# Eight row scatters spread over four attention steps with two buffers, the first expert weights copied by VectorE, and no products of zeros in the prologue

## The reference

```python
mod = (_silu(L0_c) @ L0_wmod).reshape(L0_c.shape[0], 6, 1, -1)
sa, ca, ga, sb, cb, gb = (mod[:, 0], mod[:, 1], mod[:, 2], mod[:, 3], mod[:, 4], mod[:, 5])
h = _layernorm(x, axis=-1) * (1 + ca) + sa
x = x + ga * _L0_attn_ref(h, Wq, Wk, Wv, Wo, gamma, beta)      # causal softmax, 16 heads of 8
h = _layernorm(x, axis=-1) * (1 + cb) + sb
# ffn: bids = sigmoid(h @ conf_w.T + conf_b) * wealth; the 2 best of 8 experts;
#      weights = softmax of the two bids; each expert: (silu(h @ gate.T) * (h @ up.T)) @ down.T
x = x + gb * _L0_ffn_ref(h, conf_w, conf_b, gate_w, up_w, down_w, wealth)
```

## Time and profile before

| | us |
|---|---|
| median of 3 runs | 632.87 (631.29 to 634.27) |
| the profiled execution's own time | 636.49 |
| its span | 634.7 |
| PE busy | 565.4 (89%) |
| DVE busy | 471.2 (74%) |
| ACT busy | 405.9 (64%) |
| POOL busy | 244.1 (38%) |

### The profile page before, as it was taken

One profiled execution on the slowest core, in us unless ns is written; L12 is line 12 of the kernel. 1 busy time (PEld: TensorE's weight loads), 2 busy tenths in 40 slices (PEclk: granted clock), 3 DMA queues, 4 the chain that ended last, 5 costly groups with the idle time before them and its releaser, 6 DMA issues.

```text
span 634.7 us, 16553 instructions
## 1 busy us (share of the span) xinstructions
PE 565.4 (89%) x5257; PEld 424.8 (67%) x5258; DVE 471.2 (74%) x1592; ACT 405.9 (64%) x716; POOL 244.1 (38%) x328
## 2 busy tenths in 40 slices
PE   5778999999898998998998987999888999999940
PEld 3455565666465565564564546999887999999930
DVE  5898787899797787796896863687765666667636
ACT  4425787878777786786786775686534655655612
POOL 5401301133723615416326243456554333343326
PEclk9597999999999898998998996999989999999975
DMA  4442668432333232322323011111321211111138
GB/s 125 132 121 70 176 173 224 130 110 74 95 93 93 82 93 72 103 77 71 106 82 93 3 36 27 40 44 53 103 78 53 53 50 50 42 50 50 40 124 289
DMA packets 61511, 56.82 MB, mean 90 GB/s; under 512 B 11156, under 2 KB 55572, under 8 KB 61444
## 3 DMA queue, kind: packets, MB, share of 16 engines
q1 hardware_dynamic: 56548, 44.88, 25.5%
q0 software_dynamic: 4320, 8.99, 4.3%
q10 hardware_dynamic: 576, 2.10, 0.8%
HBM read 36.92 MB, written 18.45 MB: 87 GB/s over the span
## 4 chain that ended last, share of the span: by engine, by line
PE 75%; DVE 6%; DMA 5%; issue 4%; ACT 3%; another core or an unknown queue 2%; SPq 2%; POOL 1%; ACTq 0%; POOLq 0%; DVEq 0%
PE psN L962 18%; PE psO L565 11%; PE psO L973 9%; PE psT L546 7%; PE psN L531 6%; PE psT L548 5%; PE psN L533 4%; PE psM L573 2%; ACT probs L1090 2%; DMA probs<-expert_out 2%; PE psM L591 2%; DVE negm L1408 1%; PE psM L614 1%; PE psM L596 1%
## 5 line engine op out<-in xcount | busy, mean ns | idle before, releaser
L1408 DVE TENSOR_REDUCE negm<-psN 128x1 f32<-128x512 f32 (+3 forms) x352 | 211.4, 634 | 49.6 <-PE psN L533 48.7
L1090 ACT ACTIVATE probs<-psT 128x512 f32<-128x512 f32 x320 | 179.6, 595 | 56.0 <-PE psT L548 41.0
L962 PE MATMUL psN<-probs 128*128 128x128 f32 x1136 | 142.2, 279 | 3.0 <-ACT probs L1283 2.3
L962 PEld LDWEIGHTS psN<-probs 128*128 128x128 f32 x1136 | 135.8, 196 | 3.6 <-issue 3.5
L546 PE MATMUL psT<-qst_all,kst_all 74*128 74x256 bf16 (+2 forms) x384 | 100.9, 281 | 13.4 <-ACT probs L1090 12.0
L2146 POOL DMA_INDIRECT expert_out<-kst_all,dest x71 | 69.2, 975 | 112.2 <-DVE kst_all L1914 107.6
L531 PE MATMUL psN<-kst_all,qst_all 74*128 74x256 bf16 (+2 forms) x384 | 102.2, 283 | 6.8 <-DVE negm L1408 4.1
L565 PE MATMUL psO<-probs,vaug 128*32 128x512 f32 (+3 forms) x1024 | 97.0, 458 | 0.1
L533 PE MATMUL psN<-kst_all,qst_all 117*128 117x128 bf16 x512 | 92.9, 225 | 0.0
L1283 ACT ACTIVATE probs<-gu_w 128x1024 f32 x71 | 74.9, 1056 | 25.4 <-PE psN L962 21.5
L1890 DVE TENSOR_TENSOR probs<-probs,psN 128x512 f32<-128x512 f32 x71 | 48.7, 686 | 53.0 <-PE psN L962 27.9
(11 more groups left out here) (241 smaller groups left out, 743.2 us busy)
## 6 DMA issues: line engine op xcount, KB each, us to landing
qst_all<-q_parts_dram SPq DMA_DIRECT2D x96, 96.0 KB
kst_all<-k_parts_dram SPq DMA_DIRECT2D x96, 96.0 KB
kst_all<-dispatched SPq DMA_DIRECT2D x71, 66.0 KB
q_parts_dram<-qparts SPq DMA_DIRECT2D x24, 128.0 KB, 2.4
k_parts_dram<-kparts SPq DMA_DIRECT2D x24, 128.0 KB, 1.8
xall<-in_x SPq DMA_DIRECT2D x8, 256.0 KB, 3.4
gu_w<-in_gateT SPq DMA_DIRECT2D x4, 512.0 KB, 5.1
gu_w<-in_upT SPq DMA_DIRECT2D x4, 512.0 KB, 4.9
```

The costliest lines, as they stand in the source:

```text
L962: mm = pe.matmul(bank[par][:, c * P:(c + 1) * P], ew[par][:, half, c * P:(c + 1) * P], xgT[par], start=True, stop=True)
L1090: nc.scalar.activation(probs[:, g % 2, 512 * u:512 * (u + 1)], psT[:, u % TBANKS, :], ACT.Exp, scale=SOFTMAX_SCALE).then_inc(exp_done, 1)
L1408: nc.vector.tensor_reduce(dst, src, axis=AX.X, op=ALU.max, negate=True).then_inc(nat_done, 1)
```

## The change

Five edits:

1. Eight scatters of a batch are issued at eight places over four steps, `SCATTERS`: three in step g = 3 (before unit 0, after units 4 and 8), two in step 0 of the next batch, two in step 1, one in step 2. `rows` and `slots` get a second buffer, taken in turn by batches, and `dispatched` becomes two semaphores. Of batch 5, three scatters fall into step (7, 3) and five into the head of the expert stage (j = 1, 3, 5, 7 and 9).
2. The weights of the first expert tile are copied by DVE (`first_weights`) at the end of step (7, 3); PE waits for them by `ew_first`. ACT begins with tile 1.
3. ACT's table for silu is loaded before its last `keep_values` and no longer behind it.
4. The 112 products of zeros are gone.
5. The writing of `padrows` on DVE in step (7, 3) moves from behind the second layer norm's statistics to the step's start; four small tables move into the space of `xn`, with one wait on a transpose of batch 7 that lies two batches back.

```diff
-        rows = sb("rows", [P, TB, ROW])
+        rows = [sb(f"rows{i}", [P, TB, ROW]) for i in range(2)]
-        slots = sb("slots", [P, 2, TB], I32)
+        slots = [sb(f"slots{i}", [P, 2, TB], I32) for i in range(2)]
...
+        def dispatched_before(eng, b):
+            for i in range(2):
+                eng.wait_ge(dispatched[i], 16 * 2 * TB * len(range(i, b, 2)))
...
+        SCATTERS = ((3, 0), (3, 4), (3, 8), (0, 3), (0, 9), (1, 2), (1, 9), (2, 4))
+        IN_LAST = sum(g == G - 1 for g, _ in SCATTERS)
...
-            sp.wait_ge(dispatched, 16 * 2 * TB * FULL_B)
+            dispatched_before(sp, FULL_B)
...
-            keep_running(FILL_LOAD)
             for k in range(NAT):
                 nat(0, 0, k)
-                keep_running(FILL_UNIT)
-            keep_running(FILL_MAX)
             turn_max(0, 0)
...
-                pe.wait_ge(ew_ready, j + 1)
+                if isinstance(i, int) and j == 0:
+                    pe.wait_ge(ew_first, 1)
+                else:
+                    pe.wait_ge(ew_ready, j)
...
             h_norm(B - 2, (2, 3))
+            nc.scalar.preload_act_table(ACT.Silu)
             keep_values(B - 1, 3)
...
-            nc.scalar.preload_act_table(ACT.Silu)
             act.wait_ge(ew_in, 16 * 12)
             act.wait_ge(tiles_ready, 1)
             act.wait_ge(pv_done, TB * (STEPS - 1))
-            keep_weights(0, 0)
...
+            def first_weights():
+                dve.wait_ge(ew_in, 16 * 12)
+                dve.wait_ge(pv_done, TB * (STEPS - 1))
+                e = dve.value_load(tile_w_i[0:1, 0:1], min_val=0, max_val=NX - 1)
+                V.tensor_copy(ew[0].rearrange("p k f -> p (k f)"),
+                              gu_w[:, bass.ds(e, 1)].rearrange("p o k f -> p (o k f)")).then_inc(ew_first, 1)
...
-                if has_earlier(b) and rows_of(b) is rows:
-                    hold("pool", pool, dispatched, 16 * 2 * TB * b)
+                if 2 <= b < B - 1:
+                    pool.wait_ge(dispatched[b % 2], 16 * 2 * TB * (b // 2))
...
+            def scatter_at(b, g, unit):
+                i = SCATTERS.index((g, unit))
+                sent = b - 2 if g == 3 else b - 3
+                if has_batch(sent):
+                    if unit:
+                        pool.wait_ge(exp_done, UNITS * (4 * b + g) + unit)
+                    scatter(sent, i)
...
+                if j % 2 == 1 and IN_LAST + j // 2 < 2 * TB:
+                    scatter(L - 2, IN_LAST + j // 2)
```

More of the change, by code:

```diff
@@ L320, in rows_of @@
         def rows_of(b):
-            return rows_last if isinstance(b, int) and b == B - 1 else rows
+            return rows_last if b == B - 1 else rows[b % 2]
         yp = [probs[:, b // 4, b % 4 * 2 * TB * E:(b % 4 + 1) * 2 * TB * E].rearrange("p (k n e) -> p k n e", k=2, n=TB)
@@ L327, in slots_of @@
         def slots_of(b):
[L328 removed]
+            return slots_last if b == B - 1 else slots[b % 2]
+        def dispatched_before(eng, b):
+            for i in range(2):
+                eng.wait_ge(dispatched[i], 16 * 2 * TB * len(range(i, b, 2)))
         passed = {e: sem(f"passed_{e}") for e in ("sp", "pe", "dve", "pool")}
@@ L898, in _ @@
             pe.wait_ge(ones_in, 16)
-            def keep_running(n):
-                for _ in range(n):
-                    pe.matmul(psO[:, 0:P], zero_b[:], zero_b[:], start=True, stop=True)
-            keep_running(FILL_LOAD)
             for k in range(NAT):
                 nat(0, 0, k)
-                keep_running(FILL_UNIT)
-            keep_running(FILL_MAX)
             turn_max(0, 0)
@@ new lines, in scatter @@
+                                      rows_of(b)[:, n, :], None).then_inc(dispatched[b % 2], 16)
+            def scatter_at(b, g, unit):
[5 more added lines that the diff above has]
+                    scatter(sent, i)
+            def step(b, g):
+                if g == 0:
+                    if has_batch(b - 2):
+                        h_scale(b - 2)
+                    if has_batch(b + 1) and has_earlier(b):
+                        low(b + 1, qres, qparts, q_mid, q_parts)
+                    if has_batch(b - 2):
+                        h_shift(b - 2)
+                    scatter_at(b, g, 3)
+                    if has_batch(b + 1):
+                        low(b + 1, kres, kparts, k_mid, k_parts)
+                    scatter_at(b, g, 9)
+                elif g == 1:
+                    scatter_at(b, g, 2)
+                    if has_batch(b - 1):
+                        o_inv(b - 1)
+                    if has_batch(b - 2):
+                        count(b - 2)
+                    if b == 0:
+                        x_inv(slice(2, B), 3)
+                        x_shift(slice(2, B))
+                    scatter_at(b, g, 9)
+                elif g == 2:
+                    scatter_at(b, g, 4)
+                    if has_batch(b - 1):
+                        add_attn(b - 1)
+                elif g == 3:
+                    scatter_at(b, g, 0)
+                    scatter_at(b, g, 4)
+                    if has_batch(b - 1):
+                        h_inv(b - 1)
+                    scatter_at(b, g, 8)
```

60 lines of the change are left out of this document (15 added, 45 removed).

## The result

| | before | after |
|---|---|---|
| median of 5 runs | 632.87 us | 612.76 us |
| lowest to highest | 631.29 to 634.27 | 611.86 to 614.62 |
| profiled execution, its span | 636.49, 634.7 | 611.86, 610.1 |

The ratio is 0.9686, 95% interval 0.9659 to 0.9712: 20.1 us less, where 611 was forecast. The traces are compared with each other, so their differences add up to 24.6 and not to 20.1.

A forecast was written before the change was run, and what follows sets the result against it. PE's own work was taken as the floor, with PE idle or slow-clocked behind bursts of scatters. Terms 20.1 + 4.0 - 3.6 + 1.1 = 21.6 less took the 632.87 us median to 611.3, forecast 611, range 605 to 617 (0.62).

The forecast's parts named there:

- batches 2 to 7, bursts gone: Attention: without bursts of scatters PE runs at full clock with little idle time; 20.1 us less, bounds 22.6 and 0.
- start of the expert stage, tiles 0 to 2: First expert tiles: ACT's table load and weight copy 2.0, last burst 0.7, clock 1.3; in all 4.0 us less.
- head, tiles 3 to 11, five new pairs: Expert stage's head: five of batch 5's scatters join tiles' sends there; 3.6 us more, bounds 0 and 11.
- prologue and batch 0: Prologue: without the products of zeros DVE's waits before six maxima go; 1.1 us less.
- some 3 us: Attention: the spacing of moved scatters, at least three units of exponentials apart.
- the rival of 631: Attention: the pause belongs to the place in step 3, so spacing gains nothing; 631 us, chance 0.08.
- Half a lag left: Attention: spaced scatters beside SP's loads each still hold ACT 0.5 us, giving back 9; 620 us, chance 0.15.
- Every spaced scatter costs: Attention: each of 43 moved scatters holds PE 0.72 us, 31 in all; 642 us, chance 0.05.
- the tables of `padrows` move into DVE's wait for `add_attn`, at nothing either way: Before the expert stage: moving DVE's writing of these tables neither costs nor gains time.
- a pair costs 0.72: Expert stage's head: each send with a scatter costs 0.72 us, so five new pairs cost 3.6.
- 1.1 stays as the gain: Prologue: slower products between 40 and 45 us are covered by PE's wait until 48.89, keeping the 1.1 us gain.
- the clock stays low: Behind 49 us: without zeros the clock rises later, costing 1.8 us; 613 us, inside the forecast's range, not counted apart.

The follow-up runs named there:

- the second set: Follow-up runs of before and after unchanged and of two kernels adding bursts or scatters; before took 632.7 us in its one run here, after 613.4.
- the set with pauses: The second set, whose traces show "remote" waits of ACT and DVE of up to 5.2 us, called pauses.
- the sets without pauses: The first and third sets of follow-up runs; none of their eight traces has a pause, and before took 607.9 and 607.0 us.
- e_double_narrow: Kernel after with each of 40 spaced scatters sent a second time, the second writing 64 bytes per row, not 528; 605.3 us, 0.995 of before.
- the first set: Follow-up runs undoing one part of the change at a time; the kernel before took 607.9 us (17 runs).
- e_old_places: Kernel after with each batch's scatters back at the old places in two bursts, none in the head; 602.0 us, 0.989 of before.
- e_after_again: Kernel after, unchanged, timed again in the second set; 613.4 us, 0.967 of before.
- e_scatters_only: Kernel before with only the scatters' new places and the two buffers; 600.6 us, 0.988 of before.
- e_head_free: Kernel after with batch 5's five scatters taken out of the head, all eight in step (7, 3); 599.5 us, 0.984 of before.
- e_zeros_back: Kernel after with PE's 112 products of zeros back in the prologue; 599.8 us, 0.987 of before.
- e_zeros_again: Kernel after with PE's 112 products of zeros back, a second time, in the third set of runs; 601.0 us, 0.986 of before.
- e_act_first: Kernel after with the first tile's weights copied by ACT again, behind its table load; 604.7 us, 0.995 of before.

## Why the prediction was right, and where not

| term | forecast | traces of the result | traces of the second set |
|---|---|---|---|
| batches 2 to 7, bursts gone | -20.1 | -22.4 (258.3 to 235.9) | -19.8 (255.7 to 235.9) |
| start of the expert stage, tiles 0 to 2 | -4.0 | -3.3 (11.73 to 8.42) | -2.8 (11.54 to 8.73) |
| head, tiles 3 to 11, five new pairs | +3.6 | +0.9 (32.02 to 32.88) | +0.8 (31.97 to 32.82) |
| head, tiles 12 to 29 | 0 | 0.0 (62.68 both) | 0.0 (62.76 to 62.80) |
| prologue and batch 0 | -1.1 | -0.1 (86.64 to 86.54) | +3.5 (86.33 to 89.79) |
| batch 1 | 0 | -1.0 (39.53 to 38.55) | -0.2 (38.84 to 38.64) |
| from tile 30 on | 0 | +1.3 (143.8 to 145.1) | +1.4 (143.8 to 145.2) |
| sum | -21.6 | -24.6 | -17.1 |

The two pairs of traces lie on either side of the difference of the medians (-20.1 and -20.7), so a term is known no better than the two columns agree.

**The bursts.** The reading of the earlier trace rows was right for the condition in which the kernel was timed: three or four indirect DMAs in a row are followed by pauses of ACT and DVE, one alone is not, and the pause follows the burst to another place. In the first pair the term is 2.3 us short. Batches 2 to 5 came out at 39.5 to 39.7 and not 40.1, because I left each the 0.5 us of idle time that batch 1 had; that is 1.9. Batch 6 gained 0.4 less than forecast and batch 7 0.2 more, and 0.5 lies in the stretch from 382.54 to the first tile, which the earlier trace rows left out. In the second pair the term comes out at 19.8. One reading was wrong without harm: three units of exponentials are not "some 3 us" but 2.2 at the closest (scatters at 175.28 and 177.47 in the kernel after), so 2.2 us is already far enough.

From the rule of the Trainium skill (SBUF — State Buffer, "Who interferes with whom") I had worked out that a burst on POOL could not hold ACT, which made the rival of 631. In the set with pauses ACT waits behind the burst, wherever it stands, so that rival has fallen. Whether SBUF's ports have a part in it no run shows, and in the sets without pauses nothing speaks against the rule.

**Half a lag left** did not happen: PE stands at most 0.05 us a batch in batches 2 to 5. **Every spaced scatter costs** did not either: 0.50 us each was the point where it decides, and e_double_narrow ran sixteen a batch in 39.40 us, though in a set without pauses; with them it is the kernel after, with eight a batch in 39.52 to 39.71, that excludes it.

**The start of the expert stage.** The sum came near, -3.3 and -2.8 for -4.0, but partly by luck. PE's wait for ACT's copy is gone and the products ran at the full clock, as forecast. The step that failed is "the tables of `padrows` move into DVE's wait for `add_attn`, at nothing either way": they hold up the statistics, through them ACT's last norm, and behind it the `oT` for which PE waits 0.60. The wait that was to take them in (2.72 us ahead of the statistics at 378.03) came from the burst that stood before `add_attn` on POOL, and went with it: after, the statistics wait for nothing but DVE's own work. ACT's copy for tile 1, which I had named as late next, costs 0.21. DVE costs the most: its statistics of the attention's output stand ahead of the tile copy, 1.16 us at tile 2. Where edits 2, 3 and 5 can be seen apart from the rest, in the first set, they are worth 0.7 and not the 3.3 of their two terms (2.0 for ACT's copy, 1.3 for the clock). What is left of the measured gain would lie with the last burst, for which I had 0.7, and with PE reaching tile 0 later for its waits in batches 6 and 7; no run shows the shares.

**The head.** Another step that failed in size: "a pair costs 0.72", worked out as the difference of two stretches. That difference is the price of indirect DMAs 1.3 us apart for 16 tiles where pauses exist, since it is nearly gone in e_old_places (52.82 for 18 tiles, 2.93 each, against 2.79 for a tile with nothing else). Five single pairs among tiles that have none make no such row, and cost 0.86 in all, 0.78 of it at tile 11 through the late count.

**The prologue.** DVE's gain was there: its maxima of step 0 ran without the gaps of the earlier trace rows. It was lost again before batch 1, and in the second pair 3.5 us more than that. The step that failed is "1.1 stays as the gain": I looked for the price of the missing zeros up to PE's wait at 48.89 only. The stretch where it went, in the kernel after, and a part of it:

```profile
70.00:86.50 16.50, 15.90 (x154) 8.86 (x151) 11.71 (x25) 12.54 (x26) 0.00 (x0) 0.90 0.54 135
76.70:80.10 3.40, 3.40 (x19) 1.69 (x12) 0.83 (x3) 1.62 (x4) 0.00 (x0) 0.50 0.80 218
```

PE stands 0.6 for the row maxima's DMA, and from 76.70 to 80.10 the granted clock is 0.50, that is 1.2 GHz, after a stretch at 2.4; before has 16.50 busy at 1.00 here. This is the rival "the clock stays low", at another place than I had it, and in e_after_again it costs more than the 1.8 that I gave it. Over nine traces without and five with the zeros no difference at the start of batch 2 is left. The gain in batch 1, 1.0 and 0.2, goes with the zeros too, since all nine traces without them have that batch shorter than all five with them.

**The sum.** That the total fits better than its terms is luck. In the first pair bursts 2.3 and batch 1 1.0 more than forecast, the head 2.7 less dear, against prologue 1.0, expert start 0.7 and the end 1.3. The end's 1.3 lies behind the last send: from tile 69 on it is 34.9 before, 36.1 after; both traces of the second set repeat it (34.9 and 36.2). All traces but those of the kernel before have at least 36.1, e_scatters_only and e_old_places (36.2 both) among them. So it is neither the places of the scatters nor edits 2, 3 and 4. What all these kernels share is two buffers, two semaphores and the tables moved into `xn`; which of them it is stays open.

And the 20 us are not a constant of the change. They hold where the pauses exist (0.969 and 0.967, measured twice). In the sets without pauses the kernel after itself was not timed. Its near relatives lie at 0.984 to 0.988 of before: e_head_free, e_zeros_back, e_zeros_again, e_scatters_only. None of them can be told from the kernel after in the set in which that one was timed, so no version is shown to beat it.

## What to carry to other kernels

When an engine waits for a result that the trace shows as finished, look on the other engines for a row of indirect DMAs whose last starts some 2 us before the engine goes on; pull them apart (2.2 us was enough here, 1.27 was not, and nothing between was tried), and check on POOL's own timeline that its other work doesn't close them up again. Price such a repair in the condition of the chip in which it is measured, and put the kernel before into every set of runs: here the same program took 608 and 634 us, and the gain was 3.2% where pauses are and 1.2 to 1.6% for the near relatives where none are. And before moving work to where an engine seems idle, look for what stands behind it there: the tables of `padrows` were to fill a wait of DVE's, but the same change took that wait away, and POOL and ACT then waited behind the tables. And price a pair by tiles like those in which it will stand, not by an average over a crowded stretch.

## What the runs showed of the hardware

- Indirect DMAs of 128 rows of 528 bytes take POOL 0.95 to 1.22 us each in either condition. With pauses, rows of three or four of them 1.27 us apart were followed in most batches by 2.3 to 4.3 us of waiting on ACT or 1.6 to 2.4 on DVE; without, never.
- A wait of PE of 3.85 us was followed by products at half speed (3.75 for sixteen, e_act_first), one of 2.14 by 3.18 (e_scatters_only), one of 0.48 by 2.01 (after).
- A scratch array in DRAM, written in attention and read by nothing, made the end of the kernel from tile 69 on 4 us longer in all three kernels that have it (40.1 to 40.2 against 36.1 and 36.2). In that stretch they run what the kernel after runs; the cause was not tested.
